# Setup of a channel-grouping kernel: raw images turned by products with diagonals of 1 / norm, instead of transposes of normalised images

## The reference

```
x_flat = x.reshape(B, C, H * W)
nrm = jnp.linalg.norm(x_flat, axis=2, keepdims=True)
x_n = x_flat / jnp.maximum(nrm, 1e-12)
cos = jnp.einsum('bcn,bdn->cd', x_n, x_n) / B
_, idx = jax.lax.top_k(-jnp.abs(cos).T, k)          # k = 2
s, sq = x.sum(axis=(2, 3)), (x * x).sum(axis=(2, 3))
gs = s + s[:, idx[:, 1:]].sum(axis=-1)              # the same for gsq
mean = gs / N; var = gsq / N - mean * mean          # N = k * H * W
x_hat = (x - mean) * rsqrt(var + EPS)               # then gamma and beta
```

## Time and profile before

| | us |
|---|---|
| median of 3 runs | 433.67 |
| lowest and highest | 433.36, 436.99 |
| the profiled execution | 431.37 |
| its span | 429.0 |
| busy: TensorE products | 396.0 (92%) |
| busy: TensorE weight loads | 347.7 (81%) |
| busy: ScalarE | 327.7 (76%) |
| busy: VectorE | 318.9 (74%) |
| busy: GpSimd | 111.6 (26%) |

### The profile page before, as it was taken

How to read it: one execution, slowest core, us unless ns; L and a number is a source line. 1 busy time by engine, 2 the same in 40 slices (tenths; PEclk the granted TensorE clock), 3 DMA queues, 4 the chain that set the end, 5 groups by cost and what they waited for, 6 DMA issues and landing times.

```text
span 429.0 us, 19043 instructions
## 1 busy us (share of the span) xinstructions
PE 396.0 (92%) x7707; PEld 347.7 (81%) x7707; DVE 318.9 (74%) x897; ACT 327.7 (76%) x419; POOL 111.6 (26%) x241
## 2 busy tenths in 40 slices
PE   4878899999999999999987899999999998999970
PEld 4755798999999999988865698999999897998860
DVE  4659878788888878886429878888888786787435
ACT  2527788888888888887726788888888887878745
POOL 6202323223332322237001322322222222220000
PEclk9999999999999999999999999999999999999995
DMA  7300322321112222232000232332222222223005
GB/s 222 86 2 11 76 59 51 36 57 36 37 34 47 44 46 44 46 47 40 3 2 4 56 71 37 41 48 44 44 45 44 44 47 47 49 48 40 2 3 196
DMA packets 59405, 20.80 MB, mean 48 GB/s; under 512 B 51680, under 2 KB 59184, under 8 KB 59360
## 3 DMA queue, kind: packets, MB, share of 16 engines
q1 hardware_dynamic: 54464, 17.73, 21.3%
q0 software_dynamic: 4896, 2.43, 2.2%
HBM read 3.28 MB, written 2.10 MB: 13 GB/s over the span
## 4 chain that ended last, share of the span: by engine, by line
PE 83%; DVE 6%; ACT 4%; issue 2%; DMA 2%; POOL 2%; SPq 0%; DVEq 0%; ACTq 0%; POOLq 0%
PE acc_ps L708 56%; PE z_ps L681 13%; PE build_ps L664 8%; PE side_ps L624 2%; PE side_ps L613 2%; POOL moved L270 2%; DMA xs<-in_x 1%; ACT raw L534 1%; ACT S L461 1%; DVE bstats L806 1%; PE acc_ps L569 1%; PE side_ps L602 1%; PE build_ps L559 1%; DMA moved<-conv_sb 0%; DVE raw L798 0%
## 5 line engine op out<-in xcount | busy, mean ns | idle before, releaser
L708 PE MATMUL acc_ps<-S,Z 64*64 64x256 f32 x4608 | 287.6, 377 | 1.2 <-ACT S L474 0.9
L708 PEld LDWEIGHTS acc_ps<-S,Z 64*64 64x64 f32 x4608 | 225.8, 133 | 26.3 <-issue 3.7
L461 ACT ACTIVATE S<-build_ps,minus 128x1024 f32<-128x1024 f32 x190 | 201.3, 1111 | 29.7 <-PE build_ps L664 29.3
L681 PE MATMUL z_ps<-wz,xflat 64*64 64x192 f32 x1536 | 104.3, 328 | 0.0
L664 PE MATMUL build_ps<-feat_rows,cst 64*64 64x512 f16 x576 | 79.4, 377 | 3.9 <-ACT S L461 2.7
L454 ACT ACTIVATE Z<-z_ps 128x768 f32<-128x768 f32 x96 | 78.1, 813 | 5.4 <-PE z_ps L681 5.4
L681 PEld LDWEIGHTS z_ps<-wz,xflat 64*64 64x64 f32 x1536 | 73.8, 132 | 6.5 <-issue 0.9
L270 POOL DMA_DIRECT2D moved<-conv_sb x140 | 71.3, 517 | 21.5 <-POOL conv_sb L360 15.6
L940 DVE TENSOR_SCALAR S<-build_ps 128x512 f32<-128x512 f32 x96 | 65.6, 683 | 14.9 <-PE build_ps L664 14.8
L942 DVE TENSOR_SCALAR S<-build_ps 128x512 f32<-128x512 f32 x96 | 65.2, 679 | 0.0
L947 DVE COPY raw<-acc_ps 128x256 f32 (+1 forms) x32 | 13.6, 424 | 62.1 <-PE acc_ps L708 62.1
(11 more groups left out here) (106 smaller groups left out, 286.7 us busy)
## 6 DMA issues: line engine op xcount, KB each, us to landing
xs<-in_x SPq DMA_DIRECT2D x4, 512.0 KB, 6.6
out<-raw SPq DMA_DIRECT2D x7, 256.0 KB, 2.6
moved<-conv_sb POOLq DMA_DIRECT2D x56, 11.2 KB, 1.7
moved<-conv_sb SPq DMA_DIRECT2D x56, 11.2 KB
moved<-conv_sb POOLq DMA_DIRECT2D x56, 11.3 KB, 1.6
wz<-in_dcn_w POOLq DMA_DIRECT2D x2, 288.0 KB, 4.5
feat_rows<-feats SPq DMA_TRANSPOSE x30, 3.7
moved<-conv_sb SPq DMA_DIRECT2D x28, 12.0 KB
```

What stands on the lines that cost most here:

```text
L461: act.activation(S[:, (parity + b) % 2, half, 0:ACT_TAPS, :], build_ps[:, 0:ACT_TAPS, :], ACT.Relu, bias=minus2[:, :], scale=1.0 if half = ...
L681: mm = pe.matmul(z_ps[halves[c], i, h * BLOCK_COLS:(h + 1) * BLOCK_COLS], xflat[parity][halves[i], pixels], wz[halves[i], layer, h, b * BL ...
L708: mm = pe.matmul(acc_ps[halves[i], g, 0:HW], Z[halves[g], slot, i, half, j * C:(j + 1) * C], S[halves[g], slot, half, j, :].rearrange(by_i ...
```

## The change

TensorE now turns the raw images and normalises them in the same step. For every pair of images VectorE writes two diagonal matrices of 64x64 with 1 / norm of each channel (`diags`, in `raw`; one instruction for the four pairs of a quarter, from `fold` and `rinv` with spread operands). A product with the 128 pixels of one image's 64 channels as weights and the diagonal as the streamed operand gives pixels by normalised channels. A step j has eight such products, in tiles of 64 rows by 128 columns, the two images in different row tiles and different PSUM banks; even steps write `build_ps`, odd ones `z_ps`. Each is fp32, so two instructions. The products with x are in the order of the code below.

ScalarE takes the sum of squares of two of the four pairs of a quarter (`Square` with a sum along the row), VectorE that of the other two by `bn_stats` as before. The statistics of ScalarE's pairs, which are still needed for the plain sums, are taken by VectorE at the end of the setup's loop, and all plain sums by one instruction. ScalarE's order is written out by hand. It also takes a square root of a constant before anything else. The constant block has `fold` first, loaded where the identity was, and the identity comes with the rest; VectorE waits for `fold` at the very start. `keep_busy(10)` is `keep_busy(4)`, with `fold`, and `keep_busy(6)` is `keep_busy(5)`.

The partner of each channel is added to the row's half (0 or 64), spread over 128 columns by the same instruction, multiplied with the identity on TensorE, which lays the partners of all rows along the columns, and compared with the row's number when the identity is added. The clearing of `pick` and the numbers 0 to 63 are gone; `minus2` is set first. The load of `wc` is issued after the third quarter of x has come.

```diff
+        diags = raw[:, :, 0:C]
+        turned_x = (build_ps[:, 0:2, 0:HW], z_ps[:, :, 0:HW])
...
             pool.wait_ge(x_in[X_CHUNKS - 2], 16)
+            pool.dma_start(wc[:, :, :], conv_w).then_inc(weights_in, 16)
...
+            def square(g):
+
+                act.wait_ge(x_in[g], 16)
+                for t in range(g * CHUNK_PAIRS + DVE_PAIRS, (g + 1) * CHUNK_PAIRS):
+                    act.activation(raw[:, t, :], xs[:, t, :], ACT.Square, accum_out=sums[:, 1, t:t + 1]).then_inc(squared, 1)
...
+            act.wait_ge(cleared, 1)
+            act.activation(batch_std[:, :], minus2[:, :], ACT.Sqrt, scale=-0.5)
+            square(0)
             norm(0)
...
+            copy_turned(0)
+            square(1)
+            norm(1)
+            copy_turned(1)
+            square(2)
+            norm(2)
+            copy_turned(2)
+            copy_turned(3)
+            square(3)
+            norm(3)
+            for j in range(4, PAIRS // 2):
+                copy_turned(j)
...
-            keep_busy(10)
+            keep_busy(4)
 
             def turn(j):
-                if j == PAIRS // 2 - 1:
-                    pe.wait_ge(xn_by_dve, 2 * (X_CHUNKS + 1))
-                else:
-                    pe.wait_ge(xn_by_act if j % 2 else xn_by_dve, 2 * (j // 2 + 1))
+
+                pe.wait_ge(diags_ready, j // 2 + 1)
                 if j >= 2:
                     pe.wait_ge(xn_t_ready, j - 1)
-                for i in range(2):
+                for t in range(2):
                     for h in range(HALVES):
-                        q = 2 * i + h
-                        mm = pe.transpose(build_ps[:, j % 2, q * P:(q + 1) * P],
-                                          xn[:, 2 * j + i, h * P:(h + 1) * P], ident)
+                        for i in range(2):
+                            mm = pe.matmul(turned_x[j % 2][:, i, (2 * t + h) * C:(2 * t + h + 1) * C],
+                                           xs[halves[i], 2 * j + t, h * P:(h + 1) * P], diags[halves[i], 2 * j + t, :],
+                                           start=True, stop=True)
                 mm.then_inc(xn_turned, 1)
...
+                    dve.tensor_tensor(diags[:, chunk, :], fold[:, 0:C].unsqueeze(1).broadcast_to([P, CHUNK_PAIRS, C]),
+                                      rinv[:, chunk].unsqueeze(2).broadcast_to([P, CHUNK_PAIRS, C]),
+                                      ALU.mult).then_inc(diags_ready, 1)
+
+            parts = bstats[:, :, :].rearrange("p t (e s) -> p t e s", e=2)
+            dve.wait_ge(fold_in, 16)
             for g in range(X_CHUNKS):
+                mine = slice(g * CHUNK_PAIRS, g * CHUNK_PAIRS + DVE_PAIRS)
+                if g == 1:
+                    for part in range(3):
+                        invert_norms(0, part)
                 dve.wait_ge(x_in[g], 16)
...
+            for part in range(3):
+                invert_norms(X_CHUNKS - 1, part)
+            for g in range(X_CHUNKS):
+                for t in range(g * CHUNK_PAIRS + DVE_PAIRS, (g + 1) * CHUNK_PAIRS):
+                    ins = dve.bn_stats(bstats[:, t, :], xs[:, t, :])
+            ins.then_inc(late_stats, 1)
+            dve.wait_ge(late_stats, 1)
+            dve.tensor_tensor(sums[:, 0, :], parts[:, :, 0, 1], parts[:, :, 1, 1], ALU.add).then_inc(sums_ready, 1)
             dve.wait_ge(gram_step, PAIRS // 2)
...
-            dve.tensor_copy(partner[:, :], top8_at[:, GROUP - 1:GROUP]).then_inc(setup_dve, 1)
...
-                dve.tensor_scalar(pick[rows, rows], iota[rows, :], partner[rows, :], None, ALU.is_equal).then_inc(setup_dve, 1)
...
+            dve.tensor_scalar(partner[:, :], top8_at[:, GROUP - 1:GROUP].broadcast_to([P, P]), half_row, None,
+                              ALU.add).then_inc(setup_dve, 1)
             dve.wait_ge(gram_step, PAIRS // 2 + 2)
-            dve.tensor_tensor(pick_t[:, :], side_ps[:, 1, 0:P], ident, ALU.add).then_inc(setup_dve, 1)
+            dve.scalar_tensor_tensor(out=pick_t[:, :], in0=side_ps[:, 1, 0:P], scalar=row, in1=ident,
+                                     op0=ALU.is_equal, op1=ALU.add).then_inc(setup_dve, 1)
```

More of the change, by code:

```diff
@@ L48 @@
 CHUNK_PAIRS = PAIRS // X_CHUNKS
+DVE_PAIRS = CHUNK_PAIRS // 2
 GROUP = 2
@@ L77 @@
 BN_OPS = 7
-CONST_SIZES = dict(ident=P, fold=P, combine=2 * SLICE_PLACES, combine_taps=SLICE_PLACES, grid=PLACES, iota=C, edges=2)
+CONST_SIZES = dict(fold=P, ident=P, combine=2 * SLICE_PLACES, combine_taps=SLICE_PLACES, grid=PLACES, row=1, half=1, edges=2)
 CONST_ENDS = list(accumulate(CONST_SIZES.values()))
@@ L153, in program @@
         top8_at = sb("top8_at", [P, 8], U32)
-        partner = sb("partner", [P, 1])
-        pick = sb("pick", [P, P])
+        partner = sb("partner", [P, P])
         pick_t = sb("pick_t", [P, P])
@@ L186, in program @@
         evens = cst16[:, 3 * P:CONST16_COLS].rearrange("p (n e) -> p n e", e=2)
-        iota = cst[:, CONSTS["iota"][0]:CONSTS["iota"][1]]
+        row = cst[:, CONSTS["row"][0]:CONSTS["row"][1]]
+        half_row = cst[:, CONSTS["half"][0]:CONSTS["half"][1]]
         taken = feats[:, :, 0:BLOCK_TAPS, :]
@@ L202, in program @@
         stat_step = sem("stat_step")
+        squared = sem("squared")
+        late_stats = sem("late_stats")
         sums_ready = sem("sums_ready")
@@ L580, in _ @@
             pe.matmul(side_ps[:, 0, 0:C], fold, gram_sb[:, :], start=True, stop=True).then_inc(gram_step, 1)
[L581 to L585, removed]
+            keep_busy(5)
+            pe.wait_ge(setup_dve, 6)
+            pe.matmul(side_ps[:, 1, 0:P], partner[:, :], ident, start=True, stop=True).then_inc(gram_step, 1)
+            pe.wait_ge(setup_dve, 7)
+            pe.wait_ge(sums_ready, 1)
             pe.matmul(side_ps[:, 0, 0:2 * PAIRS], pick_t[:, :], sums[:, :, :].rearrange("p a t -> p (a t)"),
@@ L783, in _, with invert_norms @@
         def _(dve):
-            def normalise(g, part):
+            def invert_norms(g, part):
                 chunk = slice(g * CHUNK_PAIRS, (g + 1) * CHUNK_PAIRS)
@@ L811, in _ @@
-                parts = bstats[:, chunk, :].rearrange("p t (e s) -> p t e s", e=2)
+                for t in range(mine.start, mine.stop):
+                    ins = dve.bn_stats(bstats[:, t, :], xs[:, t, :])
+                ins.then_inc(stat_step, 1)
+                if g >= 2:
+                    invert_norms(g - 1, 0)
                 dve.wait_ge(stat_step, 4 * g + 1)
-                dve.tensor_tensor(squares[:, chunk, :], parts[:, :, :, 1], parts[:, :, :, 1], ALU.mult).then_inc(stat_step, 1)
+                dve.tensor_tensor(squares[:, mine, :], parts[:, mine, :, 1], parts[:, mine, :, 1], ALU.mult).then_inc(stat_step, 1)
@@ L814, in _ @@
+                if g >= 2:
+                    invert_norms(g - 1, 1)
                 dve.wait_ge(stat_step, 4 * g + 2)
-                dve.scalar_tensor_tensor(out=squares[:, chunk, :], in0=squares[:, chunk, :], scalar=HW / 2.0,
-                                         in1=parts[:, :, :, 2], op0=ALU.mult, op1=ALU.add).then_inc(stat_step, 1)
+                dve.scalar_tensor_tensor(out=squares[:, mine, :], in0=squares[:, mine, :], scalar=HW / 2.0,
+                                         in1=parts[:, mine, :, 2], op0=ALU.mult, op1=ALU.add).then_inc(stat_step, 1)
@@ L817, in _ @@
+                if g >= 2:
+                    invert_norms(g - 1, 2)
                 dve.wait_ge(stat_step, 4 * g + 3)
[L818 to L821, removed]
+                dve.tensor_tensor(sums[:, 1, mine], squares[:, mine, 0], squares[:, mine, 1], ALU.add).then_inc(stat_step, 1)
@@ L1060, in shape_constants @@
     put("grid", PLACE_SCALE * grid.reshape(P, -1))
-    put("iota", np.arange(C))
+    put("row", part[:, None])
+    put("half", part[:, None] // C * C)
     edges = np.ones((P, 2), np.float32)
```

66 lines of the change are left out of this document (20 added, 46 removed).

## The result

The changed kernel takes 446.0 us (median of 4 runs, 444.11 to 447.25) where the kernel before takes 433.51 (430.28 to 436.99 over 4): a ratio of 1.0279, 95% interval 1.0235 to 1.0324. It is slower, and 5 us beyond the range of the prediction. The profiled execution took 445.04, its span 443.2 against 429.0, 14.2 longer.

The account below looks back on a forecast made before the run. TensorE's turns and grams were taken to bound the setup before the first pad at 26.39. Plus 2.0 to the gram and minus 0.3 for the partner gave plus 1.7 us: median 435.3, range 431.3 to 440.6.

Parts of the forecast that it names:

- 3, the clock: Setup's start: first turn at the low level, high level between 9.5 and 12; as late as 14 costs 1.0 us.
- Rival C: Setup's turns: thin streaming keeps the clock low, steps of turn and gram double; 444 us, chance 0.06.
- The turn (1): TensorE's turn: eight pairs 0.112 apart, 0.99 us against 0.59; a loop step from 1.20 to 1.60.
- B: Turns: the two halves of a pair load in turn, 0.224 a pair, 5.3 us over six; 440.6 us, chance 0.13.
- A: Turns: weight loads wholly hidden, 0.059 a pair, 2.6 us saved in all; 432.7 us, chance 0.16.
- rival D: Turns: load and product add in the same tile, 0.43 a turn, 2.8 us in all; 438.1 us, chance 0.05.
- The start (2): VectorE's work before the first turn: diagonals take 0.43; first turn at 7.5 instead of 9.80, 2.3 us earlier.
- ScalarE's order (4): ScalarE before the second turn: first copy, two squares to 10.95, diagonals at 12.0, where turn 2 starts.
- The sum at the high clock (5): From turn 2 to the gram: turns 1.60 apart, gram taken at 22.5 instead of 20.53, plus 2.0 us.
- The late statistics (6): VectorE's end of the setup loop: 2.9 us from about 17.2 to 20.1, hidden by turns 5 to 7.
- The partner (7): Between gram and first pad: one add replaces cast and comparisons, a product replaces the transpose; sum minus 0.3 us.
- E: ScalarE: Square throws out Sqrt's table, up to seven more loads of 1.28 us; 440 to 442 us, chance 0.03.

Follow-up runs that it names:

- e5: The changed kernel with keep_busy(20) instead of keep_busy(4) at the start, a longer warm-up; ratio 1.0388 to the kernel before.
- e9: The changed kernel with keep_busy(6), twelve instructions, added between every turn and gram; ratio 1.0261 to the kernel before.
- e3: The changed kernel with each product of a turn streaming its diagonal twice, 128 columns instead of 64; 434.98 us, ratio 1.0056 to the kernel before.
- e7: The kernel before, transposes kept, with two of four sums of squares on ScalarE, late statistics, later wc load, the new partner part, keep_busy(6); ratio 0.9990.
- e2: The kernel before with keep_busy(4) instead of keep_busy(10) at the start, nothing else; ratio 1.0044.
- e6: The kernel before with only the partner part of the change: one add, one product, one comparison; ratio 1.0019.
- e10: e7 with three of the eight late statistics moved into VectorE's wait for the square root; ratio 0.9941 to the kernel before.
- e4: The changed kernel with turns of four full-tile products, diagonals of 128x128 with zeros between images, identity loaded first; ratio 1.0063 to the kernel before.
- e1: The changed kernel with keep_busy(10) instead of keep_busy(4) at the start; ratio 1.0354 to the kernel before.
- e8: The changed kernel with keep_busy(2), four instructions, added between every turn and gram; 455.05 us, ratio 1.0497 to the kernel before.

## Why the prediction was wrong

The step that failed is 3, the clock. It took the high level to come "somewhere from 9.5 to 12" and bounded the delay at 14, 1.0 us. It took for granted that a TensorE without gaps gets the high clock. In the changed kernel the low level lasted from the first product into the first convolution, behind 39.55: a step of 2.95 instead of 1.60, the gram at 30.91 instead of 22.5. The profile before could not contradict the step, as the long stretches of its setup are at 128 streamed columns for 128 loaded, or 64 for 64. Rival C named the right mechanism, down to "the pairs stream 0.05 of each 0.11", and gave it 0.06. It was also the case of the largest price, and the range left it out.

C's price of 8.8 us was good up to the gram, which came 8.4 behind the forecast of 22.5. What it lacked is that filler products sit on the same clock: it priced 0 for `keep_busy(5)` and `keep_busy(9)`, which take 2.24 and 4.00. In the span C would be 10.5 us (1.7 and 8.8) and 14.2 were measured. The 3.7 between them are 0.4 less up to the gram, 1.1 more from there to the pad (plus 0.8 for minus 0.3), 1.2 from the pad to the first convolution product, and 1.8 behind that. On the medians C's 444 is 2 us short.

The other steps, one by one:
- The turn (1): pairs step side by side, not in turn. e5 has 0.94 and 0.99 at the high level, e9 1.04. B would have been 1.9, A 0.6; at the high level neither happened. The changed kernel's turn of 1.90 (12.22 to 14.12) is B's sign by the number, but comes from the clock, as the gram beside it shows. Load and product do not add up in a tile either (rival D, a turn of 1.42).
- The start (2): 7.5 was 7.56; the diagonals took 0.42 for 0.43.
- ScalarE's order (4): two squares with their reads took 0.90 (10.07 to 10.97) for 0.85; the read of the sum is an instruction of its own of 0.19. The diagonals were ready at 12.13 for 12.0. That turn 2 started at 12.22, near the forecast, is luck: TensorE was at the slow gram until then, and not this path but the clock set the start. In e3, at the high level, turn 2 does wait for the diagonals, to 12.36.
- The sum at the high clock (5): e3 shows it, with its turn 0.1 longer for the doubled streaming: gram 23.5, pad 29.1, against 22.5 and 28.1; six times 0.11 is two thirds of that. Its measured ratio of 1.0056 is plus 2.4 us, the forecast was plus 1.7.
- The late statistics (6): 2.9 us as said, from 19.67 and not 17.2, with 8.3 us of waiting behind them; where the gram is early, in e7, they are the bound, as said.
- The partner (7): minus 0.2 for minus 0.3, as the comparison takes 0.36 and not 0.29.
- One table load was in the profile, so not E.
- "Behind 26.39 no instruction is changed" held for the code, not for the time: from the pad to the end it is 405.6 us instead of 402.6. Of the 3.0 the clock explains 1.6 (1.2 up to the first convolution product and 0.4 in it).

The Trainium skill, in "TensorE: Matmul & The Clock Gate", section "What's actually happening", puts the level down to how busy the engine has been. The busy time of the records does not tell the level here: in e5 it is 14.00 of 14.00 us with the granted clock at 0.50. The rule of Part 3 of that page, that a load overlaps a running product only in another row group, did not hold here either: by rival D's sum it gives a turn of 1.42, and turns took 0.94 to 1.04.

Open: behind the first pad, where all kernels have the same code, the rest took 402.6 us in the kernel before, and 402.8 to 404.7 in the runs with an early high clock (e2, e6, e7, e10, e3, e4). e3 and e4, at the high level, are 1.6 and 2.1 longer there, so that part is not the clock of the setup. No run separates what sets it. The fall of the clock in the first layer in e1, e5 and e8 (from 62.1, 63.2 and 68.3 us) is open too; it is not in the changed kernel's profile, though TensorE waits 1.19 us there ahead of 60.60. In e5:

```profile
63.00:67.00 4.00, 4.00 (x52) 0.57 0.12 31
```

## What to carry to other kernels

A tuned stretch of TensorE's work has a clock behind it, and a replacement with fewer streamed columns per loaded column can lose it even if TensorE is hardly ever idle: compare the two before counting instructions, and price the filler and everything after at the low level too. If a product must be thin, streaming its operand twice costs little while loading is the bound: here 0.1 us in a turn, against about 10 us gained. And a case that is unlikely but far dearer than the others belongs in the text with its full price, and that price should be made with all that shares its cause.

## What the runs showed of the hardware

- Products that stream 64 columns for 128 loaded do not bring up a low clock: in e5 0.50 for 14.00 busy us, in the changed kernel a step of 2.95 to the last. The same products streaming 128 columns do: in e3 the gram at 11.26 is at the high level.
- A clock that was high fell in e5 from 1.00 to 0.50 at about 15.5 us, behind two such turns, a gram and a wait of 1.15 us; whether the products or the wait did it is not shown.
- The granted clock reads 1.00 up to the first change of level in the records, also where the spacing is that of the low level (5 to 8 us before, 5 to 40 us after).
- Two row tiles of 64x128 load side by side: a turn of sixteen loads of 128 columns and their products takes 0.94 to 1.04 us at the high level; e4's turn of eight, one behind the other in the full tile, takes 1.09.
- A sum along the row on ScalarE is a second instruction of 0.19 us; two squares of 128x256 with their sums follow in 0.90.
